# Another order for the opening of attention and for the casts of its keys

## The chip, the cores and the metric

The kernel runs on 1 core of one Trainium2 chip. The metric is the time of one execution in microseconds (us).

## What is computed

A block of three parts on x (4 batches, 128 tokens, width 512): cross attention over a context of 2048 tokens with 16 heads of 32, a gated scan, and a mixture of experts. The change is in the first part:

```python
q = x.reshape(B, T, H, d) * scale          # x is layer-normed; B 4, T 128, H 16, d 32
k = cond_k.reshape(B, S, H, d) * scale     # S 2048; keys and values are the same context
v = cond_v.reshape(B, S, H, d)
scores = jnp.einsum('bthd,bshd->bhts', q, k)
w = jax.nn.softmax(scores.astype(jnp.float32), axis=-1).astype(scores.dtype)
out = jnp.einsum('bhts,bshd->bthd', w, v).reshape(B, T, W)
return out @ w_proj.T + b_proj
```

## The kernel before

Attention works on 16 groups, one for each batch and block of four heads. A group's keys (1 MB, float32, `kt`, two buffers) are split into two float16 parts: ACT casts the high part (`kh`, two halves of two heads, `split_keys` at L433), and POOL subtracts it from the keys for the low part (`kl`, four heads, one instruction each, L608). DMAs from one place of SBUF to another then stack them for the matmuls, rows high, low, high, 32 rows each, in one of three stacks (`stacks[j % 3]`): six copies of 128 KB for each half `h` of the 2048 keys, so twelve for a group. The third stack lies in `wst[:, 1]`, where expert weights go later.

For each group PE then makes 16 matmuls of unscaled scores (`max_scores`, L1013) whose maxima DVE takes (L720; L772 for group 0); DVE makes the shift out of them; PE transposes queries with the shift in them (`shifted`, L1027), ACT copies them (`take_shifted`, L455); PE makes the scores in eight steps (`scores`, L1035), ACT the exponents (`exponent`, L470, four buffers), POOL sums each pair of key tiles (`pair_sum`, L632), and PE adds up values (`values`, L1049) and denominators from the pair sums (`denominators`, L1064).

Every engine has its own order, written out by hand, and waits on semaphores. All of them go in groups i of four quarters p of two steps each. In quarter p of group i PE makes maxima of group i+1 (in the last quarter of group i+2), scores of steps 2p+2 and 2p+3, which reach into the next group in the last quarter, then denominators of the two steps before the current ones, and values of steps 2p and 2p+1. `shifted(i+1)` stands on PE before the last quarter. ACT makes the exponents of PE's scores, in quarter 1 `take_queries(i+2)`, in quarter 2 `take_shifted(i+1)`, in quarter 3 `queries_high(i+3)`. ACT's casts of group i+3 stand in quarters 0 and 1 (in group 0: those of group 2 there, those of group 3 in quarters 2 and 3), and POOL's subtracts after pair sums 3 and 5 (in group 0: 5 and 7). For group 0 DVE makes the low parts of three heads, and for group 2 too, in the middle of its maxima (`low_parts`, L754).

Exponent n waits for `values(n-4)` and pair sum n-4, pair sum n for `denominators(n-4)`, scores n for exponent n-2. A cast of group j waits for its keys and for the copies of stack j-2; the high copies of a half wait for both casts, and from group 3 on for the scores that read the stack before; the low copies wait for POOL's last subtract of the group.

SP issues all these DMAs in one order. In the opening it issues first tokens, first keys, the identity, two rows of ones for the stacks, and the other tokens once the first keys are there; then the copies of stack 0, of which ACT issues the four high ones of half 1; then second keys, values of group 0, and so on.

Of the kernel before, what the change touches and what calls it, by code (L numbers as in the profile page):

```python
# [82 lines left out]
def build_program(nc, t, out):  # L83
# [240 lines left out]
    def stack_rows(eng, j, h, src, rows):  # L324
        for row in rows:
            for q in (2 * h, 2 * h + 1):
                eng.dma_start(stacks[j % 3][row:row + HD, :, q * S // 4:(q + 1) * S // 4],
                              src[q * HD:(q + 1) * HD, j % 2, :, :]).then_inc(k_rep[j % 3][h], 16)

    @blk.sync  # L330
    def _(sp):
        def load_k(j):
            if j >= 2:
                sp.wait_ge(split_lo, j - 1)
                sp.wait_ge(lo_dve, 2 * min(j // 2, 2))
            sp.dma_start(kt[:, j % 2, :, :], t["keysT"][j]).then_inc(kt_in[j % 2], 16)
# [6 lines left out]
        def copies(j, h, src, rows):  # L343
            stack_rows(sp, j, h, src, rows)

        def stack(j, h):
            sp.wait_ge(split_hi, 2 * j + 2)
            if j >= 3:
                sp.wait_ge(st_done, HS * (j - 3) + HS // 2 * (h + 1))
            copies(j, h, kh, (0, 2 * HD))  # L350
            sp.wait_ge(split_lo, j + 1)
            if j == 2:
                sp.wait_ge(lo_dve, 4)
            copies(j, h, kl, (HD,))
# [3 lines left out]
        sp.dma_start(idh[:, :], t["idh"]).then_inc(id_in, 16)  # L358
        sp.dma_start(kstk[KS:KM, :, :, :], t["ones"]).then_inc(ones_in, 16)
        sp.dma_start(stacks[2][KS:KM, :, :], t["ones"][:, 0, :, :]).then_inc(ones_in, 16)  # L360
        sp.wait_ge(kt_in[0], 16)
        sp.dma_start(x[:, 1:B, :], t["x"][:, 1:B, :]).then_inc(x_in, 16)
        sp.wait_ge(split_hi, 2)
        copies(0, 0, kh, (0, 2 * HD))
        sp.wait_ge(lo_dve, 2)
        sp.wait_ge(split_lo, 1)
        copies(0, 0, kl, (HD,))
        copies(0, 1, kl, (HD,))
        load_k(1)
        load_v(0)  # L370
        stack(1, 0)
        load_k(2)
        stack(1, 1)
        load_k(3)
        load_v(1)
        stack(2, 0)
        stack(2, 1)
        for i in range(G):
            if i + 4 < G:
                load_k(i + 4)  # L380
            if 0 < i < G - 1:
                load_v(i + 1)
            if i + 3 < G:
                stack(i + 3, 0)
                stack(i + 3, 1)
            if i == G - 3:
                for dst, name in CONSTS:
                    sp.dma_start(dst, t[name]).then_inc(consts, 16)
            if i == G - 2:
                for m in range(3):  # L390
                    sp.dma_start(wst[:, 0, m, :, :], t["ffw"][0, m]).then_inc(w_in[0][m], 16)
# [40 lines left out]
    def _(act):  # L432
# [51 lines left out]
        act.wait_ge(split_hi, 2)  # L484
        stack_rows(act, 0, 1, kh, (0, 2 * HD))
        queries_high(0)
        queries_high(1)
        take_queries(0)
# [3 lines left out]
        for h in range(2):  # L492
            split_keys(1, h)
# [4 lines left out]
        for i in range(G):  # L498
            for p in range(HS // 2):
                for n in scores_in(i, p):  # L500
                    exponent(n)
                if p == 1 and i + 2 < G:
                    take_queries(i + 2)
                if i == 0 and p < 2:
                    split_keys(2, p)
                if p in ((2, 3) if i == 0 else (0, 1)) and i + 3 < G:
                    split_keys(i + 3, p % 2)
                if p == 2 and i + 1 < G:
                    take_shifted(i + 1)
                if p == 3 and i + 3 < G:  # L510
                    queries_high(i + 3)
# [95 lines left out]
    def _(pool):  # L607
        def split_keys(j, a):  # L608
            if a % 2 == 0 or j in (0, 2):
                pool.wait_ge(split_hi, 2 * j + a // 2 + 1)  # L610
            low = pool.tensor_tensor(kl[:, j % 2, a, :], kt[:, j % 2, a, :], kh[:, j % 2, a, :], ALU.subtract)  # L611
            if a == HG - 1:
                low.then_inc(split_lo, 1)
# [11 lines left out]
        split_keys(0, HG - 1)  # L625
        queries_low(0)
        queries_low(1)
        for a in range(HG):
            split_keys(1, a)
# [15 lines left out]
        for i in range(G):  # L645
            for hs in range(HS):
                pair_sum(HS * i + hs)
                if i == 0 and hs == 4:
                    split_keys(2, HG - 1)
                if hs in ((5, 7) if i == 0 else (3, 5)) and i + 3 < G:  # L650
                    for a in ((0, 1) if hs == (5 if i == 0 else 3) else (2, 3)):
                        split_keys(i + 3, a)
                if hs == HS - 1 and i + 3 < G:
                    queries_low(i + 3)
# [49 lines left out]
    def _(dve):  # L704
# [49 lines left out]
        def low_parts(j, h):  # L754
            dve.wait_ge(split_hi, 2 * j + h + 1)
            heads = (slice(0, 2), slice(2, 3))[h]
            dve.tensor_tensor(kl[:, j % 2, heads, :], kt[:, j % 2, heads, :], kh[:, j % 2, heads, :], ALU.subtract)\
                .then_inc(lo_dve, 1)

        low_parts(0, 0)  # L760
        low_parts(0, 1)
# [23 lines left out]
        for i in range(G):  # L785
            if i == G - 1:
                scale_win()
            for p in range(HS // 2):
# [9 lines left out]
                if p in (1, 2) and i == 0:  # L798
                    low_parts(2, p - 1)
# [566 lines left out]
```

## Time and profile before

| | us |
|---|---|
| median of 3 runs | 535.68 |
| lowest and highest | 532.35, 535.93 |
| the profiled execution | 537.27 |
| its span in the profile | 535.5 |

| engine | busy us | share of the span |
|---|---|---|
| PE (matmuls) | 468.8 | 88% |
| DVE | 401.7 | 75% |
| ACT | 329.7 | 62% |
| POOL | 290.4 | 54% |

Attention ends at about 290 us, so POOL's busy time lies nearly all in the first 55% of the span. The profiled execution took 1.8 us more than the span, which begins with the first instruction and ends with the last.

### The profile page before, as it was taken

Reading aid. Unit: us, or ns where it says so; the run is one execution under the profiler, and the core shown is the slowest. Engines: PE = TensorE matmul, PEld = TensorE weight load, DVE = VectorE, ACT = ScalarE, POOL = GpSimd, SP = SyncE. Lnnn points to the kernel's source line nnn. Section 1 sums busy time; section 2 is a strip of 40 time slices with the busy share of each in tenths; the row PEclk is TensorE's granted clock in tenths of the full one; section 3 lists DMA queues with packets and bytes.
Section 4 is the critical chain, followed back from the end, with each engine's and each line's share of the span. In section 5 each row is a group of like instructions: output and inputs, shape, how many; then the busy total and the mean of one; then the engine's idle time right before and its main releaser. Section 6 shows DMA issues by size and latency. Waiting matters only on the chain.

```text
span 535.5 us, 15785 instructions
## 1 busy us (share of the span) xinstructions
PE 468.8 (88%) x6731; PEld 329.2 (61%) x6731; DVE 401.7 (75%) x598; ACT 329.7 (62%) x362; POOL 290.4 (54%) x274
## 2 busy tenths in 40 slices
PE   0468887999999999999989955999999999999994
PEld 0126555676666766667666532844878788787642
DVE  3467665787877788787771799698599999999426
ACT  3327465776767777776654373456579888788320
POOL 2045698899999999999769430482001101010042
PEclk9999898999999999999999996999999999999998
DMA  7986799878888987987992731076999999997125
GB/s 201 239 194 202 194 257 273 241 206 223 248 255 251 265 255 188 256 223 183 359 375 97 295 97 61 1 253 232 416 355 412 416 420 416 417 417 319 40 85 171
DMA packets 48253, 133.97 MB, mean 250 GB/s; under 512 B 6452, under 2 KB 31284, under 8 KB 37428
## 3 DMA queue, kind: packets, MB, share of 16 engines
q1 hardware_dynamic: 43928, 120.38, 69.3%
q0 software_dynamic: 3680, 12.06, 6.2%
q8 instruction: 53, 0.87, 0.7%
q10 hardware_dynamic: 576, 0.52, 0.5%
q14 instruction: 16, 0.13, 0.1%
HBM read 96.77 MB, written 11.01 MB: 201 GB/s over the span
## 4 chain that ended last, share of the span: by engine, by line
PE 45%; DVE 34%; DMA 8%; issue 8%; ACT 2%; POOL 2%; SPq 1%; DVEq 0%; ACTq 0%; POOLq 0%
DVE mx L720 11%; DVE ws L805 9%; PE bank L1059 8%; PE bank L1024 8%; PE bank L1068 6%; PE bank L1044 6%; DMA wst<-in_ffw 5%; PE bank L1186 2%; PE bank L1188 2%; DVE rden L737 2%; PE bank L1187 2%; DMA kstk<-kl 2%; DVE hf L946 1%; PE bank L1129 1%; DVE hl L951 1%
## 5 line engine op out<-in xcount | busy, mean ns | idle before, releaser
L720 DVE TENSOR_REDUCE mx<-bank 128x1 f32<-128x512 f32 x240 | 152.7, 686 | 60.2 <-PE bank L1024 60.0
L475 ACT ACTIVATE pt<-bank 128x1024 f32<-128x1024 f32 x128 | 126.0, 1023 | 70.8 <-PE bank L1044 69.5
L636 POOL TENSOR_TENSOR ps<-pt 128x512 f32<-128x512 f32 x128 | 159.8, 1275 | 14.8 <-PE bank L1068 9.2
L805 DVE SCALAR_TENSOR_TENSOR ws<-wst,ws 128x2048 f16<-128x2048 f32 x51 | 115.6, 2286 | 2.6 <-ACT ws L523 2.4
L523 ACT ACTIVATE ws<-wst 128x2048 f16<-128x2048 f32 x48 | 90.5, 1904 | 5.9 <-DMA wst<-in_ffw 5.7
L611 POOL TENSOR_TENSOR kl<-kt,kh 128x512 f16<-128x512 f32 x58 | 67.4, 1185 | 27.4 <-ACT kh L440 27.4
L1201 PE MATMUL bank<-xt,ws 128*128 128x128 f16 x480 | 81.2, 219 | 1.1 <-DVE hf L946 1.1
L1202 PE MATMUL bank<-xt,ws 128*128 128x128 f16 x480 | 81.2, 219 | 0.0
L1203 PE MATMUL bank<-xt,ws 128*128 128x128 f16 x480 | 81.2, 219 | 0.0
L1024 PE MATMUL bank<-kstk,q 96*128 96x512 f16 x176 | 66.6, 420 | 15.6 <-DMA kstk<-kl 7.5
L677 POOL DMA_DIRECT2D ys_rows<-xn x15 | 8.1, 543 | 121.7 <-ACT xn L592 121.7
L1059 PE MATMUL bank<-pt,v 128*32 128x128 f32 x2048 | 69.5, 277 | 2.9 <-issue 2.9
L1059 PEld LDWEIGHTS bank<-pt,v 128*32 128x32 f32 x2048 | 58.5, 112 | 3.7 <-issue 3.1
L1044 PEld LDWEIGHTS bank<-q,kstk 98*128 98x128 f16 x704 | 47.5, 101 | 15.9 <-issue 4.1
L1044 PE MATMUL bank<-q,kstk 98*128 98x128 f16 x704 | 55.7, 225 | 1.7 <-ACT pt L475 1.0
L1201 PEld LDWEIGHTS bank<-xt,ws 128*128 128x128 f16 x480 | 46.8, 98 | 2.0 <-DVE hf L946 2.0
L1203 PEld LDWEIGHTS bank<-xt,ws 128*128 128x128 f16 x480 | 46.9, 98 | 0.0
L1202 PEld LDWEIGHTS bank<-xt,ws 128*128 128x128 f16 x480 | 46.9, 98 | 0.0
L1068 PE MATMUL bank<-ps,ones 128*32 128x128 f32 x1024 | 41.8, 279 | 2.0 <-POOL ps L636 2.0
L440 ACT ACTIVATE kh<-kt 128x1024 f16<-128x1024 f32 x32 | 33.5, 1053 | 10.5 <-DMA kt<-in_keysT 10.5
L1024 PEld LDWEIGHTS bank<-kstk,q 96*128 96x128 f16 x176 | 15.3, 101 | 39.1 <-DVE mx L720 21.1
L1068 PEld LDWEIGHTS bank<-ps,ones 128*32 128x32 f32 x1024 | 24.1, 109 | 17.9 <-issue 12.2
(170 smaller groups left out, 719.0 us busy)
## 6 DMA issues: line engine op xcount, KB each, us to landing
wst<-in_ffw SPq DMA_DIRECT2D x51, 1024.0 KB, 11.0
kt<-in_keysT SPq DMA_DIRECT2D x16, 1024.0 KB, 6.3
v<-in_vals SPq DMA_DIRECT2D x16, 1024.0 KB, 9.7
kstk<-kh SPq DMA_DIRECT2D x84, 128.0 KB, 3.3
kstk<-kl SPq DMA_DIRECT2D x44, 128.0 KB, 2.8
wst<-kh SPq DMA_DIRECT2D x40, 128.0 KB, 2.8
xs_rows<-biases SPq DMA_DIRECT2D x15, 256.0 KB, 3.0
x_tok<-xs_rows POOLq DMA_DIRECT2D x15, 256.0 KB, 8.5
```

Source lines behind the costliest of these rows:

```text
L475: act.activation(pt[:, n % 4, :, :, :].rearrange("p j a t -> p (j a t)"), bank[:, 2 * (n % 2):2 * (n % 2) + 2, :].rearrange("p j n -> p (j ...
L523: act.activation(ws[:, home_of(q), 0, m, :, :].rearrange("p c n -> p (c n)"), wst[:, q % 2, m, :, :].rearrange("p c n -> p (c n)"), ACT.Co ...
L636: pool.tensor_tensor(ps2[:, n % 4, :, :], pt[:, n % 4, 0, :, :], pt[:, n % 4, 1, :, :], ALU.add)\
L720: dve.tensor_reduce(mx[:, a, q:q + 1], bank[:, 4 + k % 2, :], AX.X, ALU.max).then_inc(m_taken, 1)
L805: dve.scalar_tensor_tensor(ws[:, home_of(q), 1, m, :, :].rearrange("p c n -> p (c n)"), wst[:, q % 2, m, :, :].rearrange("p c n -> p (c n) ...
L1024: pe.matmul(bank[:, home, :], q1[:, j % 2, a, :], stacks[j % 3][0:KS, a, q * 512:(q + 1) * 512], start=True, stop=True).then_inc(m_ready, 1)
L1044: mm = pe.matmul(bank[:, 2 * (n % 2) + j, a * P:(a + 1) * P], stacks[i % 3][:, a, tile * P:(tile + 1) * P], q2[:, i % 2, a, :], start=True ...
L1059: mm = pe.matmul(bank[a * HD:(a + 1) * HD, 6 + i % 2, 0:P], v[:, i % 2, tile, a * HD:(a + 1) * HD], pt[:, n % 4, j, a, :], start=(tile == ...
L1068: mm = pe.matmul(bank[a * HD:(a + 1) * HD, 6 + i % 2, P:2 * P], ones[:, :], ps2[:, n % 4, a, :], start=False, stop=(hs == HS - 1), skip_gr ...
L1201: pe.matmul(o, ws[:, home, 0, m, c, part], xt[:, k % 2, c, :], start=(c == 0), stop=False)
L1202: pe.matmul(o, ws[:, home, 0, m, c, part], xt[:, k % 2, C + c, :], start=False, stop=False)
L1203: mm = pe.matmul(o, ws[:, home, 1, m, c, part], xt[:, k % 2, c, :], start=False, stop=(c == C - 1))
```

## The change

- SP: the other tokens and the second keys are issued right behind the first keys and the identity, with no wait. Then come the copies of stack 0, all twelve from SP, half 0 whole before half 1; then the rows of ones, the third keys, and the stacks, values and keys that follow. ACT issues no copies.
- Group 0's low parts: all four heads by DVE, two at a time. Group 1's and group 2's: all by POOL, before the first pair sum.
- ACT: the casts of group 1 come before `take_queries(0)`, those of group 2 before `take_shifted(0)`. In the groups, the casts of group i+3 come in quarter 2, behind `take_shifted(i+1)`, and in quarter 3, behind the exponents, in group 0 as in all.
- POOL: the subtracts of group i+3 come after pair sums 5 and 7.
- SP in the groups: values of group i+2 between the two halves of stack i+3, instead of values of group i+1 ahead of them. The constants go out three at a time in groups 4 to 7, and the first expert's weights in groups 8 to 10, instead of in groups 13 and 14.

```diff
@@ -321,18 +321,13 @@
     blk = block.__enter__()
 
 
-    def stack_rows(eng, j, h, src, rows):
-        for row in rows:
-            for q in (2 * h, 2 * h + 1):
-                eng.dma_start(stacks[j % 3][row:row + HD, :, q * S // 4:(q + 1) * S // 4],
-                              src[q * HD:(q + 1) * HD, j % 2, :, :]).then_inc(k_rep[j % 3][h], 16)
-
     @blk.sync
     def _(sp):
         def load_k(j):
             if j >= 2:
-                sp.wait_ge(split_lo, j - 1)
-                sp.wait_ge(lo_dve, 2 * min(j // 2, 2))
+                sp.wait_ge(split_lo, j - 2)
+            if j == 2:
+                sp.wait_ge(lo_dve, 2)
             sp.dma_start(kt[:, j % 2, :, :], t["keysT"][j]).then_inc(kt_in[j % 2], 16)
 
         def load_v(j):
@@ -341,54 +336,52 @@
             sp.dma_start(v[:, j % 2, :, :], t["vals"][j]).then_inc(v_in[j % 2], 16)
 
         def copies(j, h, src, rows):
-            stack_rows(sp, j, h, src, rows)
+            for row in rows:
+                for q in (2 * h, 2 * h + 1):
+                    sp.dma_start(stacks[j % 3][row:row + HD, :, q * S // 4:(q + 1) * S // 4],
+                                 src[q * HD:(q + 1) * HD, j % 2, :, :]).then_inc(k_rep[j % 3][h], 16)
 
         def stack(j, h):
             sp.wait_ge(split_hi, 2 * j + 2)
             if j >= 3:
                 sp.wait_ge(st_done, HS * (j - 3) + HS // 2 * (h + 1))
             copies(j, h, kh, (0, 2 * HD))
-            sp.wait_ge(split_lo, j + 1)
-            if j == 2:
-                sp.wait_ge(lo_dve, 4)
+            if j == 0:
+                sp.wait_ge(lo_dve, 2)
+            else:
+                sp.wait_ge(split_lo, j)
             copies(j, h, kl, (HD,))
 
         sp.dma_start(x[:, 0, :], t["x"][:, 0, :]).then_inc(x0_in, 16)
         load_k(0)
         sp.dma_start(idh[:, :], t["idh"]).then_inc(id_in, 16)
+        sp.dma_start(x[:, 1:B, :], t["x"][:, 1:B, :]).then_inc(x_in, 16)
+        load_k(1)
+        stack(0, 0)
+        stack(0, 1)
         sp.dma_start(kstk[KS:KM, :, :, :], t["ones"]).then_inc(ones_in, 16)
         sp.dma_start(stacks[2][KS:KM, :, :], t["ones"][:, 0, :, :]).then_inc(ones_in, 16)
-        sp.wait_ge(kt_in[0], 16)
-        sp.dma_start(x[:, 1:B, :], t["x"][:, 1:B, :]).then_inc(x_in, 16)
-        sp.wait_ge(split_hi, 2)
-        copies(0, 0, kh, (0, 2 * HD))
-        sp.wait_ge(lo_dve, 2)
-        sp.wait_ge(split_lo, 1)
-        copies(0, 0, kl, (HD,))
-        copies(0, 1, kl, (HD,))
-        load_k(1)
+        load_k(2)
+        stack(1, 0)
         load_v(0)
-        stack(1, 0)
-        load_k(2)
         stack(1, 1)
         load_k(3)
+        stack(2, 0)
         load_v(1)
-        stack(2, 0)
         stack(2, 1)
         for i in range(G):
             if i + 4 < G:
                 load_k(i + 4)
-            if 0 < i < G - 1:
-                load_v(i + 1)
             if i + 3 < G:
                 stack(i + 3, 0)
+            if i + 2 < G:
+                load_v(i + 2)
+            if i + 3 < G:
                 stack(i + 3, 1)
-            if i == G - 3:
-                for dst, name in CONSTS:
-                    sp.dma_start(dst, t[name]).then_inc(consts, 16)
-            if i == G - 2:
-                for m in range(3):
-                    sp.dma_start(wst[:, 0, m, :, :], t["ffw"][0, m]).then_inc(w_in[0][m], 16)
+            for dst, name in CONSTS[3 * i - 12:3 * i - 9] if 4 <= i < 8 else []:
+                sp.dma_start(dst, t[name]).then_inc(consts, 16)
+            if 8 <= i < 11:
+                sp.dma_start(wst[:, 0, i - 8, :, :], t["ffw"][0, i - 8]).then_inc(w_in[0][i - 8], 16)
         sp.wait_ge(st_done, HS * (G - 1))
         for m in range(3):
             sp.dma_start(wst[:, 1, m, :, :], t["ffw"][2, m]).then_inc(w_in[1][m], 16)
@@ -481,16 +474,16 @@
         for h in range(2):
             split_keys(0, h)
         root(ln1_var, 1, 0, 1)
-        act.wait_ge(split_hi, 2)
-        stack_rows(act, 0, 1, kh, (0, 2 * HD))
         queries_high(0)
         queries_high(1)
+        for h in range(2):
+            split_keys(1, h)
         take_queries(0)
         take_queries(1)
         root(ln1_var, B, 1, B)
         act.activation(r1[:, 1, 0:2], eps[:, :], ACT.Exp)
         for h in range(2):
-            split_keys(1, h)
+            split_keys(2, h)
         take_shifted(0)
         exponent(0)
         exponent(1)
@@ -501,12 +494,10 @@
                     exponent(n)
                 if p == 1 and i + 2 < G:
                     take_queries(i + 2)
-                if i == 0 and p < 2:
-                    split_keys(2, p)
-                if p in ((2, 3) if i == 0 else (0, 1)) and i + 3 < G:
-                    split_keys(i + 3, p % 2)
                 if p == 2 and i + 1 < G:
                     take_shifted(i + 1)
+                if p >= 2 and i + 3 < G:
+                    split_keys(i + 3, p - 2)
                 if p == 3 and i + 3 < G:
                     queries_high(i + 3)
 
@@ -606,7 +597,7 @@
     @blk.gpsimd
     def _(pool):
         def split_keys(j, a):
-            if a % 2 == 0 or j in (0, 2):
+            if a % 2 == 0:
                 pool.wait_ge(split_hi, 2 * j + a // 2 + 1)
             low = pool.tensor_tensor(kl[:, j % 2, a, :], kt[:, j % 2, a, :], kh[:, j % 2, a, :], ALU.subtract)
             if a == HG - 1:
@@ -622,11 +613,11 @@
             pool.wait_ge(xs_hi, j + 1)
             pool.tensor_tensor(z[:, :, 2 * HD:KS], q, z[:, :, 0:HD], ALU.subtract).then_inc(xs_lo, 1)
 
-        split_keys(0, HG - 1)
         queries_low(0)
         queries_low(1)
-        for a in range(HG):
-            split_keys(1, a)
+        for j in range(1, 3):
+            for a in range(HG):
+                split_keys(j, a)
         queries_low(2)
 
         def pair_sum(n):
@@ -645,10 +636,8 @@
         for i in range(G):
             for hs in range(HS):
                 pair_sum(HS * i + hs)
-                if i == 0 and hs == 4:
-                    split_keys(2, HG - 1)
-                if hs in ((5, 7) if i == 0 else (3, 5)) and i + 3 < G:
-                    for a in ((0, 1) if hs == (5 if i == 0 else 3) else (2, 3)):
+                if hs in (5, 7) and i + 3 < G:
+                    for a in range(hs - 5, hs - 3):
                         split_keys(i + 3, a)
                 if hs == HS - 1 and i + 3 < G:
                     queries_low(i + 3)
@@ -751,14 +740,11 @@
 
         dve.wait_ge(x0_in, 16)
         first_norm(0, 1)
-        def low_parts(j, h):
-            dve.wait_ge(split_hi, 2 * j + h + 1)
-            heads = (slice(0, 2), slice(2, 3))[h]
-            dve.tensor_tensor(kl[:, j % 2, heads, :], kt[:, j % 2, heads, :], kh[:, j % 2, heads, :], ALU.subtract)\
+        for h in range(2):
+            heads = slice(2 * h, 2 * h + 2)
+            dve.wait_ge(split_hi, h + 1)
+            dve.tensor_tensor(kl[:, 0, heads, :], kt[:, 0, heads, :], kh[:, 0, heads, :], ALU.subtract)\
                 .then_inc(lo_dve, 1)
-
-        low_parts(0, 0)
-        low_parts(0, 1)
         dve.wait_ge(roots, 1)
         link(dve.reciprocal(lnv[:, 2, 0:1], lnv[:, 0, 0:1]))
         first_normed(0)
@@ -795,8 +781,6 @@
                     first_normed(i // C + 1)
                 if p == 2 and i + 1 < G:
                     shift(i + 1)
-                if p in (1, 2) and i == 0:
-                    low_parts(2, p - 1)
         invert(G - 1)
         divide(G - 1)
```

## Rows read from the trace of the kernel before

**Rows 1.** Chain of waits: start us, us, what (`values(8i+2)` of groups 1, 4, 5, 13)
```profile
68.20 0.87 PE bank L1059 x32
...
120.02 0.87 PE bank L1059 x32
...
135.22 0.87 PE bank L1059 x32
...
256.75 0.87 PE bank L1059 x32
```

**Rows 2.** Windows: stretch, length, busy us (count) of PE PEld DVE ACT POOL, PEclk, DMA
```profile
131.00:146.19 15.19, 14.53 (x292) 10.45 (x284) 12.53 (x24) 11.14 (x14) 14.90 (x14) 1.00 0.84 241
```

**Rows 3.** Timeline, one steady group: start us, us, engine, line, operation
```profile
129.81 4.96 POOL L636 TENSOR_TENSOR ps<-pt 128x512 f32<-128x512 f32 x4
...
130.87 1.06 PE L1059 MATMUL bank<-pt,v 128*32 128x128 f32 x32
...
134.57 0.65 PE L1068 MATMUL bank<-ps,ones 128*32 128x128 f32 x16
134.73 2.46 POOL L611 TENSOR_TENSOR kl<-kt,kh 128x512 f16<-128x512 f32 x2
...
135.03 1.06 PE L1059 MATMUL bank<-pt,v 128*32 128x128 f32 x32
...
139.62 2.27 POOL L611 TENSOR_TENSOR kl<-kt,kh 128x512 f16<-128x512 f32 x2
...
139.88 0.60 ACT L459 ACTIVATE q<-bank 98x512 f16<-98x512 f16 x1 [0.78 <-PE bank L1031]
...
141.86 2.49 POOL L636 TENSOR_TENSOR ps<-pt 128x512 f32<-128x512 f32 x2
...
142.31 1.94 ACT L475 ACTIVATE pt<-bank 128x1024 f32<-128x1024 f32 x2 [1.84 <-PE bank L1044]
...
144.63 0.42 POOL L623 TENSOR_TENSOR xs<-xn,xs 128x128 f16<-128x128 f32 x1 [0.29 <-ACT xs L467]
```

**Rows 4.** Timeline of the opening
```profile
7.31 2.00 ACT L440 ACTIVATE kh<-kt 128x1024 f16<-128x1024 f32 x2 [5.06 <-DMA kt<-in_keysT]
...
12.58 2.54 SPq L327 DMA_DIRECT2D kstk<-kl  x4
...
15.16 0.61 SPq L336 DMA_DIRECT2D kt<-in_keysT  x1
...
21.76 7.96 PE L1024 MATMUL bank<-kstk,q 96*128 96x512 f16 x16 [7.53 <-DMA kstk<-kl]
...
25.18 2.00 ACT L440 ACTIVATE kh<-kt 128x1024 f16<-128x1024 f32 x2 [5.42 <-DMA kt<-in_keysT]
...
26.32 4.49 POOL L611 TENSOR_TENSOR kl<-kt,kh 128x512 f16<-128x512 f32 x4 [12.91 <-ACT kh L440]
...
34.13 1.12 PE L1044 MATMUL bank<-q,kstk 98*128 98x128 f16 x9 [0.78 <-ACT q L459]
```

**Rows 5.** Timeline of the fill: DVE, then PE
```profile
47.14 2.18 DVE L757 TENSOR_TENSOR kl<-kt,kh 128x1024 f16<-128x1024 f32 x1
...
49.98 0.39 PE L1024 MATMUL bank<-kstk,q 96*128 96x512 f16 x1 [1.11 <-DVE mx L720]
...
52.20 0.42 PE L1031 MATMUL bank<-idh,xs 128*98 128x128 f16 x4
55.66 0.59 PE L1024 MATMUL bank<-wst,q 96*128 96x512 f16 x2 [3.04 <-issue]
...
83.77 1.73 PE L1059 MATMUL bank<-pt,v 128*32 128x128 f32 x32 [2.85 <-issue]
```

**Rows 6.** Tile `v`, 0 to 100 us: issue to landing
```profile
DMA to landing us min/median/max: 9.7/11.9/12.9
```

**Rows 7.** Windows of the opening: columns as in rows 2, the last GB/s
```profile
4.00:6.00 2.00, 0.00 (x0) 0.00 (x0) 0.88 (x2) 0.00 (x0) 0.00 (x0) 1.00 1.00 413
...
16.00:18.00 2.00, 0.00 (x0) 0.00 (x0) 1.81 (x6) 0.05 (x1) 0.00 (x0) 1.00 1.15 211
```

## The prediction

> **What bounds the kernel now.** I read the chain of waits first, then the timeline of one steady group, then the opening and the fill. From about 100 us to 267 us the chain repeats the same lines each group. The 32 value matmuls of one place, `values(8i+2)`, start at 120.02 us for group 4 and at 256.75 us for group 13: (256.75 - 120.02) / 9 = 15.19 us per group [rows 1]. For group 1 the same place is at 68.20 us, so the twelve groups from 1 to 13 took 188.55 us where 12 x 15.19 = 182.3 would do. Thus 6.3 us of fill losses lie in groups 1 and 2. In a steady group PE is busy 14.53 us and POOL 14.90 us of 15.19 [rows 2]: two engines nearly full, and whatever makes one wait for the other lengthens the group. In the timeline of such a group [rows 3] POOL does four pair sums (129.81 to 134.73), two subtracts, two sums, two subtracts, two sums, and `queries_low`. Its casts on ACT came long before, so POOL hardly waits. The opening is another matter: PE starts its first maxima at 21.76 us, 7.53 us after its last work, released by the landing of the first stack's low rows [rows 4]. In the fill PE stands idle 3.04 us at 55.66 (the third stack's copies are late) and 2.85 us at 83.77 (values of group 2 loaded late) [rows 5].
>
> **The loop that the change closes (the steady groups).** This is the dear part. After the change ACT casts the first half of group i+3 behind `exponent(8i+6)`, `exponent(8i+7)` and `take_shifted(i+1)`; before, these casts stood in quarters 0 and 1. POOL's first two subtracts stand behind pair sum 5 and wait for that cast, and behind them are queued sums 6 and 7, two more subtracts, `queries_low` and the next group's sums. PE's denominators of the next group wait for these sums, and on PE the shifted transposes of the next group stand behind those denominators. So it comes back to the cast. I add up this loop from the rows of one steady group [rows 3]:
> - from the start of `values(8i+2)` at 135.03 to the start of `take_shifted` at 139.88: 4.85 us, PE busy throughout with matmuls that the change leaves as they are;
> - `take_shifted` 0.50 (it is listed at 0.60, and successive ACT starts overlap it a little), the cast 1.00 (two of them took 2.00 [rows 4]), the signal to POOL 0.07;
> - two subtracts 2.24 (start 139.62 to start 141.86), sums 6 and 7 2.49, two subtracts 2.24, `queries_low` 0.40, two sums of the next group 2.48 (half of 4.96);
> - the signal to PE 0.06, and the second half of the denominators 0.23 (half of 135.03 - 134.57; the first half is already done while the second sum runs), then `values` of the next group.
>
> The sum is 16.56 us; I take 16.6 against 15.19. The lower end is 16.3, if overlaps of starts save a little more. The upper end is 17.4: subtracts at 2.46 each pair as in the row at 134.73, both denominators behind the sum (0.46), ACT's pieces at full length. I stay near the low end because most rows of the loop are start-to-start distances already. With 16.6 the loop costs 12 x 1.41 = 16.9 us over groups 1 to 13 against a steady 15.19. The other users of the late pieces have room: the second cast (quarter 3) follows exponents that end at 144.25, so it is done at 145.3, before POOL asks at 146.2; `queries_low` ends at 148.8, and between the transposes that wait for it and the denominators, which wait until 151.4 anyway, PE has only three maxima and one set of scores, so a short delay there is covered.
>
> **SP's queue in the loop.** `load_v(i+2)` now stands behind the low copies of stack i+3, which wait for POOL's last subtract. On the scale of rows 3 that is 148.4 + 1.25 for two copies (half of 2.54 [rows 4]), so issue at 149.7. Its user, the first values of group i+2, comes at 130.9 + 2 x 16.6 = 164.1. A values load took 9.7 to 12.9 us to land [rows 6], so it lands by 162.6 at the latest: 1.5 us to spare, cost nil; if it took 15 us, each group would pay half of the excess, for two groups pass in between. `load_k(i+4)` has over a group of room. The constants (three a group in groups 4 to 7) and the first expert weights (groups 8 to 10) move out of a stretch where nobody waits for them into one where the queue has room: nothing either way.
>
> **The opening.** Removed: the wait of the other tokens and second keys for the first keys, ACT's four copies, DVE's share of group 2's subtracts. Added: group 2's casts and all four of its subtracts on POOL ahead of group 0, one longer subtract on DVE (two heads instead of one), whose end I leave where it is, since POOL no longer works beside it. Replayed:
> - First keys land and are cast 7.31 to 9.31 as now [rows 4]. Behind them in the queue are 0.77 MB of tokens and 1 MB of second keys. The queue moved 413 GB/s at 4 to 6 us [rows 7], which puts the second keys' end near 11.7 us and, with landing time, 12.5 to 14.
> - SP alone issues six copies of half 0 from 9.35, 0.63 us each (2.54 for four [rows 4]), so until 13.2. They stand behind the second keys, drain at about the 211 GB/s of 16 to 18 us [rows 7], 0.79 MB in 3.7 us from 11.7, and land by 16 to 17. Now twelve copies, tokens and all must land for the first maximum.
> - On ACT the second casts come ahead of `take_queries(0)`: cast at 13.5 to 15.5, queries at 16.0. Cost nil, covered by the copies; if the second keys came 1 us later it would show fully.
> - PE starts at 16.5 instead of 21.76: 5.2 us gained (bounds 3.5 and 6). Half 1 is issued by 17.0 and landed by 19.7, PE wants it 4.7 us after its start, 21.2.
> - Third keys are issued at 17.6 behind the rows of ones, and land at about 24 to 26 (the second keys took 10 us from 15.16 to the cast at 25.18 [rows 4]; fewer bytes are ahead of them now). Their casts take 2 us and stand ahead of `take_shifted(0)` on ACT, which is wanted some 0.7 us before `scores(0)`, at 28.2: covered, by as little as 0.2 us at worst. POOL's eight subtracts (4.49 for four [rows 4]) end near 30.5, before the first two exponents, for which POOL's next work waits.
>
> So `scores(0)`, now at 34.13 [rows 4], comes at 28.9.
>
> **Group 0.** DVE's subtract of 2.18 us at 47.14 goes; PE was idle 1.11 us for the maximum behind it at 49.98 [rows 5], so about 1.0 comes back. `shifted(1)`, now at 52.20 [rows 5], would be at 52.20 - 5.2 - 1.0 = 46.0. Here the new loop takes over: `take_shifted` from 46.5, cast end 48.0, subtracts 50.4, sums 52.8, subtracts 55.1, `queries_low` 55.5, two sums 58.0, denominators 58.25. The stall of 3.04 us on the third stack goes, since its subtracts end at 30.5 already; what is late instead is POOL. `values(8+2)` starts at 58.3; now it is at 68.0 on the same scale (the chain's 68.20 less the 0.19 by which the chain's 135.22 is behind the timeline's 135.03). That is 9.7 us gained by group 1. Values of group 2 are issued at about 56.5 and land by 69.4; PE wants them near 70.7, so the stall at 83.77 goes too.
>
> **The sum.** 58.3 + 12 x 16.6 = 257.5 us for group 13, against 256.75 - 0.19 = 256.56: +0.9 us. Behind that point the last three groups have no casts and the rest is untouched. The profiled execution lasted 537.27 us (span 535.5), 1.6 above the median 535.68 of the three runs; added to the median, the forecast is 536.6 us: two large effects, 16 us gained in opening and fill and 17 us lost in the loop, that nearly cancel.
>
> **The Trainium skill on one point.** The row of 4 to 6 us shows 413 GB/s with only first keys in the queue [rows 7], and no row shows two large loads of one queue started together. The Trainium skill ("DMA: Bandwidth & Descriptors", Queues, rings and completion order) says that on each DMA engine the descriptors of a ring are consumed in ring order. By that rule the first keys land as now; without it, see the third rival.
>
> **Rivals.**
> - The loop at its long end, slower. Where POOL's subtracts meet DVE work, and both denominators follow the sum, a group takes 17.1 to 17.4 us. From 17.0 on the change is over 1% slower (12 x 0.4 + 0.9 = 5.7). Price at 17.2: +8.1, so 543.8 us. For it: the subtract pair at 134.73 took 2.46 [rows 3]; against it: the later one took 2.24.
> - The loop does not bind, faster. If POOL's lag were absorbed and groups stayed at 15.19, group 13 would come at 58.3 + 182.3 = 240.6, so -16, 520 us. For it: four buffers of exponents lie between ACT and POOL; against it: every link above is an order in one engine or a wait.
> - The queue is shared, not in order. First keys, tokens and second keys end together: 2.8 MB at 413 GB/s is 6.8 us instead of 2.5, first cast 4.2 us later. Most of the opening's gain is gone, +4 or so: 540.7 us, still within 1%.
> - The second keys are later than I think and the gain of the opening halves: +2.5, 539.1 us.
>
> **Chances.** My forecast 0.40, the long loop 0.32, no loop 0.15, shared queue 0.07, late second keys 0.06. One per cent, about what a measurement of this kernel tells from no change, is 5.4 us. Faster by more: 0.15; within: 0.40 + 0.07 + 0.06 = 0.53; slower: 0.32. The range goes from 530 (a larger gain in the fill) to 546, and leaves out the case without the loop and the last of the long one.
>
> **What would show it.** The first maxima on PE near 16.5 us; no wait of 3 us at the third stack; POOL idle about 2 us before its first subtract of each group, put down to ACT's cast; that place in the chain 16.6 us apart, with `kl`, `ps` and `kh` on the chain where now maxima are. I am wrong if groups stay at 15.2, if values loads hold PE at a group's start, or if the first cast starts after 9 us.

## The result

The changed kernel takes 547.67 us (median of 6 runs) against 535.8 us: 1.022 times as long, 95% interval 1.0177 to 1.0262. The forecast was 536.6 us with a range to 546.0, so the change is slower by far more than the forecast's 0.9 us. One execution of each kernel took far longer than its others (696.35 us before, 1175.14 us changed), and the ratio is of the fast ones alone. The profiled execution of the changed kernel took 546.27 us, with a span of 544.5 against 535.5.

The chain of waits of the changed kernel, at the place that [rows 1] follow (`values(8i+2)`, now L1043; start us, us, what), in groups 1, 5, 6 and 13:

```profile
62.27 0.87 PE bank L1043 x32
...
128.43 0.87 PE bank L1043 x32
...
144.98 0.87 PE bank L1043 x32
...
266.62 0.87 PE bank L1043 x32
```

Group 1 reaches it at 62.27 us instead of 68.20 [rows 1]: the opening and the fill did gain, 5.9 us. A profile is one execution, though: in the profiles of two experiments whose opening is that of the kernel before, PE's first maxima start at 19.56 and 22.32 us instead of 21.76, so such a gain is known only to some 3 us. Then an undisturbed group takes 144.98 - 128.43 = 16.55 us instead of 15.19, and the twelve groups take 204.35 us instead of 188.55. At group 13 the changed kernel is 9.9 us behind; after that it wins 0.9 back.

The timeline of one such group shows where the time stands, to be laid beside [rows 3]:

```profile
125.48 7.59 POOL L627 TENSOR_TENSOR ps<-pt 128x512 f32<-128x512 f32 x6
...
134.71 2.27 POOL L602 TENSOR_TENSOR kl<-kt,kh 128x512 f16<-128x512 f32 x2 [1.64 <-ACT kh L433]
136.94 2.50 POOL L627 TENSOR_TENSOR ps<-pt 128x512 f32<-128x512 f32 x2
139.39 2.28 POOL L602 TENSOR_TENSOR kl<-kt,kh 128x512 f16<-128x512 f32 x2
...
133.09 0.60 ACT L452 ACTIVATE q<-bank 98x512 f16<-98x512 f16 x1 [0.78 <-PE bank L1015]
133.59 1.05 ACT L433 ACTIVATE kh<-kt 128x1024 f16<-128x1024 f32 x1
...
128.01 0.43 PE L1052 MATMUL bank<-ps,ones 128*32 128x128 f32 x8 [0.27 <-POOL ps L627]
128.25 1.06 PE L1043 MATMUL bank<-pt,v 128*32 128x128 f32 x32
```

POOL's first subtract stands idle 1.64 us for ACT's cast, which comes right behind `take_shifted`; and PE's second denominators wait for POOL's sum. Most links of the loop are in these rows: 128.25 to 133.09 is 4.84 us (4.85 in the working), the cast ends at 134.64, and 134.71 + 2.23 + 2.45 + 2.24 leads to `queries_low`. The rest of the ring is the same work as at 125.48 to 128.25, one group on.

The opening, to be laid beside [rows 4]:

```profile
7.33 2.00 ACT L433 ACTIVATE kh<-kt 128x1024 f16<-128x1024 f32 x2 [5.09 <-DMA kt<-in_keysT]
...
15.64 7.96 PE L1008 MATMUL bank<-kstk,q 96*128 96x512 f16 x16 [2.05 <-DMA kstk<-kl]
...
18.25 0.36 SPq L331 DMA_DIRECT2D kt<-in_keysT  x1
...
29.39 2.00 ACT L433 ACTIVATE kh<-kt 128x1024 f16<-128x1024 f32 x2 [12.64 <-DMA kt<-in_keysT]
...
32.02 1.87 PE L1028 MATMUL bank<-q,kstk 98*128 98x128 f16 x16 [4.79 <-ACT q L452]
```

The first cast starts at 7.33 us, as before, with 1.8 MB more in the queue behind the first keys: the queue isn't shared out. PE starts its maxima at 15.64 instead of 21.76. But the third keys, issued at 18.25, reach ACT only at 29.39, their casts hold up `take_shifted(0)`, and PE waits 4.79 us: of 6.1 us gained, 2.1 remain at `scores(0)`.

Last, four waits of PE that the engines' names don't explain (timeline of PE, "issue"; at the second one the 32 value matmuls are cut in two), and one group's window:

```profile
154.78 0.60 PE L1008 MATMUL bank<-wst,q 96*128 96x512 f16 x2 [1.84 <-issue]
...
168.57 0.83 PE L1043 MATMUL bank<-pt,v 128*32 128x128 f32 x23
170.56 0.49 PE L1043 MATMUL bank<-pt,v 128*32 128x128 f32 x9 [1.16 <-issue]
...
235.50 0.59 PE L1008 MATMUL bank<-kstk,q 96*128 96x512 f16 x2 [1.05 <-issue]
...
253.87 0.59 PE L1008 MATMUL bank<-wst,q 96*128 96x512 f16 x2 [2.53 <-issue]
```

```profile
242.13:262.11 19.98, 16.35 (x292) 11.86 (x284) 11.89 (x24) 11.11 (x15) 14.80 (x14) 0.91 0.81 204
```

Three of them stand before the first maxima on a new half stack, whose copies are late; the one at 170.56 is none of these, and the last section comes back to it. They lie in or right behind the groups in which SP issues constants (from 132 us on) or expert weights (at 217 and 233 us). The window, group 12 from one reciprocal (`invert`) to the next, is 19.98 us long, with a granted clock of 0.91: behind the wait of 2.53 us PE ran at 1.2 GHz for a while, here from 256 to 258 us, the column before the last two being the granted clock:

```profile
256.00:258.00 2.00, 2.00 (x29) 1.59 (x22) 0.00 (x0) 0.00 (x0) 1.72 (x2) 0.50 0.68 148
```

How late the queue was is told by the times from issue to landing, the last number of each line: first from 106.9 to 123.4 us, before any constant was issued, then from 208.3 to 242 us, among the weights:

```profile
kt<-in_keysT SPq DMA_DIRECT2D x1, 1024.0 KB, 8.4
kstk<-kl SPq DMA_DIRECT2D x4, 128.0 KB, 4.6
...
kt<-in_keysT SPq DMA_DIRECT2D x2, 1024.0 KB, 15.3
kstk<-kl SPq DMA_DIRECT2D x8, 128.0 KB, 7.5
```

### The profile page after: what moved, and what is told of

Same layout as the page of the kernel before. It is cut to its first block, busy times and chain, and to the rows that moved or that the text cites. A ratio compares the mean times of both kernels' runs of the same rounds, so it can differ in the third digit from the quotient of the medians.

```text
span 544.5 us, 15769 instructions
## 1 busy us (share of the span) xinstructions
PE 474.3 (87%) x6731; PEld 328.7 (60%) x6731; DVE 402.3 (74%) x596; ACT 329.4 (60%) x362; POOL 290.9 (53%) x276
## 4 chain that ended last, share of the span: by engine, by line
PE 40%; DVE 25%; POOL 11%; DMA 10%; issue 9%; SPq 3%; ACT 3%; DVEq 0%; POOLq 0%; ACTq 0%
DVE ws L789 9%; PE bank L1043 7%; DVE mx L709 6%; PE bank L1008 6%; POOL ps L627 6%; PE bank L1028 6%; PE bank L1052 5%; DMA wst<-in_ffw 5%; DMA kt<-in_keysT 3%; POOL kl L602 3%; SPq L341 2%; PE bank L1170 2%; PE bank L1171 2%; PE bank L1172 2%; DMA kstk<-kl 2%
## 5 line engine op out<-in xcount | busy, mean ns | idle before, releaser
L709 DVE TENSOR_REDUCE mx<-bank 128x1 f32<-128x512 f32 x240 | 153.9, 686 | 72.2 <-PE bank L1008 71.8
L1043 PE MATMUL bank<-pt,v 128*32 128x128 f32 x2048 | 70.2, 278 | 1.3 <-issue 1.2
L1043 PEld LDWEIGHTS bank<-pt,v 128*32 128x32 f32 x2048 | 58.9, 112 | 2.5 <-issue 1.8
L1052 PE MATMUL bank<-ps,ones 128*32 128x128 f32 x1024 | 46.1, 284 | 5.5 <-POOL ps L627 5.5
L433 ACT ACTIVATE kh<-kt 128x1024 f16<-128x1024 f32 x32 | 33.4, 1052 | 17.7 <-DMA kt<-in_keysT 17.7
L1052 PEld LDWEIGHTS bank<-ps,ones 128*32 128x32 f32 x1024 | 23.3, 110 | 26.2 <-POOL ps L627 12.3
```

Of the source, the lines that this page charges most:

```text
L709: dve.tensor_reduce(mx[:, a, q:q + 1], bank[:, 4 + k % 2, :], AX.X, ALU.max).then_inc(m_taken, 1)
L1043: mm = pe.matmul(bank[a * HD:(a + 1) * HD, 6 + i % 2, 0:P], v[:, i % 2, tile, a * HD:(a + 1) * HD], pt[:, n % 4, j, a, :], start=(tile == ...
L1052: mm = pe.matmul(bank[a * HD:(a + 1) * HD, 6 + i % 2, P:2 * P], ones[:, :], ps2[:, n % 4, a, :], start=False, stop=(hs == HS - 1), skip_gr ...
```

## The experiments

The length of group i is told by the distance of its reciprocals, `invert(i-1)` to `invert(i)`, which stand at its start and its end. In the kernel before they are 17.1 and 19.7 us for the first two and 15.19 after; in the changed one 16.5 to 16.6 up to group 12, but 18.9, 16.7, 16.1, 17.3 and 20.0 in groups 6, 7, 8, 11 and 12. The kernel before was timed again beside each set of experiments, and each ratio is to that, with medians of 536.05, 536.31, 535.93 and 536.85 us.

**Third keys ahead of the ones.** The changed kernel, with

```diff
-        ones rows (two loads)
         load_k(2)
+        ones rows (two loads)
```

> The changed kernel with the third keys issued ahead of the two rows-of-ones loads instead of behind them. Theory of the ones: their few long descriptors hold two of the DMA engines from 19.5 to some 24 us, and the third keys, which need all engines, land late (29.37 us) only for that. Then the keys land at 25 to 26 us, the first scores start at 28.7 instead of 32.02 us, and the whole is 2 to 3.5 us faster. Rival, plain backlog of stack copies in the queue: the keys move by the 1 us that they are issued earlier, and the whole by less than 1 us.

541.61 us, ratio to before 1.0065 (1.0021 to 1.0109): 6 us off the changed kernel. The keys landed after 6.1 us instead of 11.1:

```profile
23.64 2.00 ACT L433 ACTIVATE kh<-kt 128x1024 f16<-128x1024 f32 x2 [6.74 <-DMA kt<-in_keysT]
27.36 0.60 ACT L452 ACTIVATE q<-bank 98x512 f16<-98x512 f16 x1 [1.72 <-PE bank L1015]
28.11 1.87 PE L1028 MATMUL bank<-q,kstk 98*128 98x128 f16 x16 [0.78 <-ACT q L452]
```

`scores(0)` came at 28.11 us instead of 32.02. The ones are 96 KB only, but in rows of 32 and 16 KB on two partitions. The theory of the ones stands and the plain backlog falls. That the gain exceeds the 3.9 us of the opening isn't explained by it: the long groups came out shorter too in this run (17.7, 17.9 at most), though the constants were still among them: groups 1 to 12 took 200.7 us where the changed kernel's took 204.8. Why is open; the nine executions of this run are spread from 536.9 to 548.7 us.

**Constants late.** The changed kernel, with

```diff
-            for dst, name in CONSTS[3 * i - 12:3 * i - 9] if 4 <= i < 8 else []:
...
-            if 8 <= i < 11:
...
+            if i == G - 3:
+                for dst, name in CONSTS:
...
+            if i == G - 2:
+                for m in range(3):
...
```

> The changed kernel with the constants and the first expert's weights issued where they were before the change (groups 13 and 14). Theory: in the groups they push stack copies and loads back in a DMA queue that is nearly full, and cost the 5.8 us by which groups 1 to 13 exceed 12 x 16.55 us. Then every group from 1 to 13 takes 16.55 us and the whole is 5 to 6 us faster. Rival: the waits of 1 to 2.5 us in groups 6, 8, 11 and 12 come from stack copies that the loop itself makes late; then they stay and the time changes by under 1 us.

543.75 us, ratio 1.016 (1.0111 to 1.0209), 4 us faster than the changed kernel. Groups 1 to 12 took 199.4 us instead of 204.8 between the first reciprocal and the thirteenth: 5.4 us, as expected of the groups; the whole gained less than the expected 5 to 6. Single groups of 17.0 and 17.4 us stayed, against the expectation, and each holds a stop of PE inside a run of matmuls, 0.65 and 1.09 us, of which more in the last section. The profiled run began 1 us later and lost the rest behind attention.

**Casts early.** The changed kernel, with ACT's casts of groups 1 to 12 in quarters 0 and 1 and POOL's subtracts after pair sums 3 and 5 again.

```diff
+                if p in ((2, 3) if i == 0 else (0, 1)) and i + 3 < G:
+                    split_keys(i + 3, p % 2)
                 if p == 2 and i + 1 < G:
                     take_shifted(i + 1)
-                if p >= 2 and i + 3 < G:
-                    split_keys(i + 3, p - 2)
...
-                if hs in (5, 7) and i + 3 < G:
+                if hs in ((5, 7) if i == 0 else (3, 5)) and i + 3 < G:
```

> The changed kernel with the casts and subtracts of groups 1 to 12 where they were before the change (ACT quarters 0 and 1, POOL after pair sums 3 and 5); group 0 and all else as changed. Theory of the loop (cast behind take_shifted, sums behind the subtracts): groups fall from 16.55 to 15.2 us, 12 x 1.36 = 16 us faster, less up to 4 us that the constants cost more in shorter groups: 531 to 535 us. Rival, the longer groups come from the DMA queue (loads and copies late): groups stay near 16.5 us and the gain is under 3 us.

545.85 us, ratio 1.0191 (1.0116 to 1.0266): only 1.8 us gained. The rival has the number, under 3 us, but neither theory had the groups right. Groups of 15.18 and 15.19 us did appear, so the loop is gone; but beside them stood groups of 20.7, 18.7 and 20.6 us. The chain of waits names one cause in group 10:

```profile
197.31 19.22 DMA kt<-in_keysT
```

The keys of a later group took 19.22 us behind twelve copies, values and a weight, and ACT, which now casts in quarter 0, stood before them with all exponents behind it. In group 4, before any constant is issued, the cause is another:

```profile
115.92 1.05 PE L1043 MATMUL bank<-pt,v 128*32 128x128 f32 x31
119.35 0.37 PE L1043 MATMUL bank<-pt,v 128*32 128x128 f32 x1 [2.38 <-issue]
```

PE stops between the 31st and the 32nd of 32 matmuls that no wait divides. Nine such stops add up to 9.3 us in this run; I come back to them below.

**Casts late in the kernel before.** The opposite edit: the kernel before, with this part of the change alone: the diff above, its signs turned round.

> The kernel before with one part of the change alone: casts of groups 1 to 12 in ACT quarters 2 and 3 and subtracts after pair sums 5 and 7. Theory of the loop: from group 3 on each group takes 16.55 instead of 15.19 us, ten groups of 1.36 us, 13 to 15 us slower, near 549.5 us. Rival, the DMA queue: loads and constants stand as before, so the time stays near 536 us.

552.04 us, ratio 1.0238 (1.0155 to 1.0321), 16 us slower, a little more than expected. The chain repeats every 16.55 us here too:

```profile
121.19 0.87 PE bank L1059 x32
...
137.74 0.87 PE bank L1059 x32
...
154.30 0.87 PE bank L1059 x32
```

So the loop alone, with loads and constants in their old places, makes the group 1.36 us longer, 13.6 us over ten groups. Most of the rest of the 16 us lies in group 7, which took 19.6: PE waits there 2.49 us for values.

**Subtracts after sum 7.** The changed kernel, with all four subtracts of a group behind `pair_sum(8i+7)`: it shortens the loop by sums 6 and 7 without moving a cast.

```diff
-                if hs in (5, 7) and i + 3 < G:
-                    for a in range(hs - 5, hs - 3):
+                if hs == 7 and i + 3 < G:
+                    for a in range(HG):
                         split_keys(i + 3, a)
```

> The changed kernel with all four subtracts of a group after pair sum 7, so that sums 6 and 7 no longer stand behind the first cast; the casts stay late. Theory of the loop, added up from its links: take_shifted ends 6.35 us after the values of quarter 1, POOL subtracts from the first cast's end, waits for the second cast until some 10.2 us after that mark, then two subtracts, queries_low, two sums and the denominators: 15.8 to 16.0 us a group instead of 16.55, so 6 to 8 us faster than the changed kernel unless the DMA queue gives some of it back. Rival, the cast alone sets the length: 16.55 stays.

541.85 us, ratio 1.0046 (0.9996 to 1.0097). Undisturbed groups took 15.65 us, 0.15 less than the low end I had added up and 0.9 less than with the loop of the change. POOL waits for each half's cast, as the sum had it:

```profile
99.30 2.27 POOL L602 TENSOR_TENSOR kl<-kt,kh 128x512 f16<-128x512 f32 x2
102.48 2.28 POOL L602 TENSOR_TENSOR kl<-kt,kh 128x512 f16<-128x512 f32 x2 [0.91 <-ACT kh L433]
104.72 0.42 POOL L614 TENSOR_TENSOR xs<-xn,xs 128x128 f16<-128x128 f32 x1
```

The loop's length follows its links; one group of 22.2 us among the constants remained.

**Three parts undone.** The changed kernel with the diffs of three experiments together: third keys ahead, constants late, casts early.

> The changed kernel with three parts undone together: third keys ahead of the rows of ones, constants and first weights late, casts and subtracts of groups 1 to 12 early. What is left of the change is the opening, group 0, and the place of the values load between two stack halves. If the constants made the long groups (up to 20.7 us) of the early casts, groups take 15.2 to 15.5 us and the whole is 522 to 526 us. Rival, the place of the values load makes copies, keys and instruction fetches late in a group of 15.2 us: several groups stay at 17 us or more and the whole is 530 us or more.

533.14 us, ratio 0.9945 (0.9902 to 0.9988). The rival came true in the time, 530 us or more, and half way in the groups: they took 15.19 us, but also 16.4, 16.8, 17.6 and 18.5. Stops of PE inside runs of matmuls add up to 4.7 us here, a wait for copies makes 2.3.

**Constants in the groups of the kernel before.** The kernel before, with the diff of "constants late" turned round.

> The kernel before with the constants and first weights in groups 4 to 10, as in the change, and nothing else. Theory, a nearly full DMA queue: the groups of 15.19 us that get 1 MB or more in addition become longer, 3 to 8 us in all, 539 to 544 us. Rival, the queue has room (as the prediction had it): all groups stay at 15.19 and the time at 536 us.

543.43 us, ratio 1.0079 (1.0034 to 1.0125). Six groups kept 15.18 to 15.20 us; four among the loads took 19.2, 16.3, 16.8 and 16.5, and one ahead of them 16.6, with a stop of 0.96 us inside a run. The first group that took in constants, from 127.20 to 142.40 us, is among the six: 1.5 MB more went through at 307 GB/s with no loss. The loss came in the next:

```profile
144.59 1.77 PE L1057 MATMUL bank<-pt,v 128*32 128x128 f32 x32 [2.27 <-issue]
```

The values for this place were issued at 131.61, behind the constants and the keys, and took 12.9 us to land. So the queue can take 1 MB more into one group; what is issued behind it and waited for comes late.

**Only the opening.** As "three parts undone", and with the values load back ahead of both stack halves:

```diff
+            if 0 < i < G - 1:
+                load_v(i + 1)
             if i + 3 < G:
                 stack(i + 3, 0)
-            if i + 2 < G:
-                load_v(i + 2)
-            if i + 3 < G:
                 stack(i + 3, 1)
```

> As the run with three parts undone, with the values load of a group back in its old place ahead of both stack halves: SP's order in the groups is that of the kernel before, and only the opening and group 0 are changed. Theory, the place of the values load matters: groups of 15.19 us from group 1 or 2 on, the first reciprocal near 55 us instead of 63.9, two groups of fill at most 1 us too long, in all 519 to 523 us. Rival, groups become long for the shorter lead of the fill itself: then this run has long groups as well and stays above 526 us.

528.06 us, ratio 0.9833 (0.9769 to 0.9896): the fastest of all, 8 us faster than the kernel before and 20 faster than the changed one. All groups from 4 on took 15.19 us:

```profile
106.56 0.96 DVE rden L727
...
121.75 0.96 DVE rden L727
```

The steady groups are as the theory has them, but the time is on the rival's side, above 526 us. It is 5 us slower than I expected: the first reciprocal came at 57.85, not 55, and the first three groups took 3.1 us too long. It is a version that beats both kernels; it isn't the end of the road.

**Opening and loop.** The last kernel with the late casts put back.

> The run with only the opening changed (528.1 us), with the late casts and subtracts of groups 1 to 12 put back and nothing else. Theory: the loop costs 12 x 1.36 = 16.3 us by itself, whatever the queue does; every group takes 16.55 us and the time is 543 to 546 us. Rival, the loop's cost depends on loads and constants in the queue: with these in their old places the groups are shorter than 16.4 us.

544.43 us, ratio 1.0115 (1.004 to 1.019): 16.4 us more than with early casts by the medians, 14.4 without the longest of the four executions. The expected number is 16.3, but it isn't shown that the loop alone makes it. In the profiled execution, that longest one (555.4; the others took 540 to 546), most groups took 16.55 us and three took 20.6 to 22.1, which neither side had:

```profile
163.24 1.93 PE L1044 MATMUL bank<-pt,v 128*32 128x128 f32 x32 [2.22 <-issue]
```

The values for this place were issued at 153.9 and took 9.2 us: they landed at 163.1. The wait of 2.49 us in "casts late in the kernel before" is at the same place. With late casts a values load that is issued behind both halves of a stack, which is itself late, comes too late.

**Values first, in the changed kernel.** The diff of "only the opening" alone, on the changed kernel.

> The changed kernel with the values load put back in its old place, ahead of both stack halves, and nothing else. In groups of 16.55 us the queue has more room than in groups of 15.19, so if the constants alone make the long groups of the changed kernel (18.9, 20.0 us), they stay and the time moves by less than 2 us; if the place of the values load has its part in them, they shrink and 3 us or more come back.

561.24 us, ratio 1.0402 (1.0322 to 1.0483). 13.6 us slower than the changed kernel, which I had on neither side:

```profile
146.37 1.94 PE L1042 MATMUL bank<-pt,v 128*32 128x128 f32 x32 [6.72 <-issue]
```

Issued at 134.0 behind constants of 1.5 MB and keys of 1 MB, the values landed 12.3 us later, at 146.3. So the new place of the values load is what late casts need, and the old place is what early ones need; each part of the change reads differently beside the other.

**Keys first and constants late, loop kept.** The first two diffs together on the changed kernel.

> The changed kernel with third keys ahead of the rows of ones and constants late: the loop and the values load between the stack halves stay. Theory: with the values load in its new place no group waits for values (groups of 20.6 and 22.1 us in the run with late casts and values first came from that), so nearly all of groups 1 to 12 take 16.55 us, one or two up to 1 us more; the sum of both single edits, 547.7 - 6 - 4, gives 538 to 541 us. Rival, the values' place is no cure: groups of 20 us appear here too.

538.97 us, ratio 1.0043 (1.0009 to 1.0076). Nine of the first twelve groups took 16.54 to 16.56 us, the others 16.1, 17.3 and 17.4. Two of its reciprocals, in DVE's timeline:

```profile
171.22 0.96 DVE L728 RECIPROCAL rden<-bank 128x128 f32<-128x128 f32 x1 [0.35 <-PE bank L1054]
...
187.76 0.96 DVE L728 RECIPROCAL rden<-bank 128x128 f32<-128x128 f32 x1 [0.37 <-PE bank L1054]
```

With both moved loads back in better places, the change is 2 us slower than the kernel before beside it: near the +0.9 of the forecast. Two of the long groups, 17.4 and 17.3 us, hold stops of PE of 0.98 and 1.03 us inside a run.

## Why the prediction was wrong

- **The loop**: right, and to the hundredth. 16.56 us added up, 16.55 measured; 16.6 was taken. Single links are off by up to 0.05 and cancel, which is luck in the last digit. Its ends (to 17.4) were too wide: none of the dear ends applied. The rival "no loop" falls with the groups of 16.55 us, in the kernel before too once its casts are late.
- **The opening up to the maxima**: right in kind, PE at 15.64 against 16.5. Queue in order: right, 7.33 against 7.31 us before. The Trainium skill's rule ("DMA: Bandwidth & Descriptors", Queues, rings and completion order) holds here.
- **"Third keys ... land at about 24 to 26"**: this step failed. They reached ACT at 29.39. I counted bytes ahead of them, and missed that the rows of ones, now just ahead, lie on two partitions. It cost 3.1 us at `scores(0)` (32.02 against 28.9). Shown by the first experiment, which gives back 3.9 us there and, by the medians, 6 us of the whole.
- **Group 0**: `values(8+2)` came 3.8 us late. In the first experiment it comes at 59.82 us in the chain instead of 62.27, so about 2.5 of them are the keys'. The other 1.3 I can't place.
- **"The constants ... and the first expert weights move ... into one where the queue has room: nothing either way"**: this step failed. In the profiled execution the twelve groups from 1 to 13 took 204.35 us, 5.1 more than 12 x 16.6 and 5.8 more than 12 x 16.55, and the trace of "constants late" gives 5.4 back. In whole time, by the medians, the loads cost 3.9 us in the changed kernel, 2.6 beside early third keys (541.61 against 538.97) and 7.1 in the kernel before (by the ratios 3, 1 and 4). So that they cost something is shown from both sides; how much depends on what stands beside them. Nor are all 5.1 us theirs: the stop of 1.16 us in group 7 is of another kind, and with the third keys ahead the same groups took 200.7 us with the constants in them and 199.8 without.
- **How that step failed**: I looked for room in the queue and didn't ask what is waited for behind the loads. A sum of bytes wouldn't have helped. The row of windows says 0.84 of the DMA engines' time in a steady group, in its last but one column [rows 2]; 1 MB more is 2.5 us at 413 GB/s [rows 7], and 0.84 x 15.19 + 2.5 is 15.3 us, an estimate, which fits into a group of 16.55. And the groups that took a load in did fit: 16.54 us with a weight in it (from 208.29 us, 272 GB/s), 15.20 with 1.5 MB of constants in the kernel before. The loss came behind, where keys landed after 15.3 us instead of 8.4 and low copies after 7.5 instead of 4.6, and PE waited 1.84, 1.05 and 2.53 us for copies.
- **SP's queue, values load "cost nil"**: right for the change as it stands; the experiments show by how little.
- **The sum**: +0.9 us forecast at group 13, +9.9 measured; 3.8 and 5.1 make the difference. The chances put 0.47 on two rivals of the loop, which came out as added up, 0.13 on the queue in the opening, and none on the rows of ones or the constants. The rival of the long loop names a time nearer to the measured one, 543.8 us, but by groups of 17.2 us, and the undisturbed ones took 16.55: its nearness is luck.

## What to carry to other kernels

Where an engine is moved behind a wait, add up the ring of waits that it closes: that sum, from start-to-start distances in one steady group, gave the group's length here to 0.01 us. For the DMA queue such a sum of bytes isn't enough to call a load free: look at each DMA behind it that an engine waits for, how long it takes to land, and how long its user can wait. Keep small loads to few partitions behind, not ahead of, a load that is waited for. And where several parts move, test them in pairs. With third keys ahead and constants late, the four kernels took 528.06 us (casts and values load in the old places), 533.14 (values load moved), 544.43 (casts moved) and 538.97 (both moved): the new place of the values load costs 5 us beside early casts and gives 5 back beside late ones.

## What was unexpected

**Few partitions, long rows.** Two loads of 64 and 32 KB to two partitions made 1 MB behind them land in 11.1 us instead of 6.1. The trace of the changed kernel has them as two packets of 32 KB, which took 2.6 and 2.1 us, each followed with no gap by one of 16 KB, which took 1.8. I read that as two of the 16 DMA engines being held for about 4 us each, near the 5.0 us by which the keys were late.

**PE stops inside a run of matmuls.** Gaps of 0.2 to 2.4 us lie between matmuls with no wait between them, at 23 + 9 of 32 in the changed kernel and at the same place in four of the experiments. The profile's DMA queues list one of kind "instruction" with 53 packets. In "casts early", in the stretch from 107.3 to 128 us around the stop of 2.38 us, it moved three packets beside a full data queue:

```profile
q1 hardware_dynamic: 2218, 4.43, 97.1%
q8 instruction: 3, 0.05, 1.2%
```

One of the three went from 116.63 to 117.92 us, and PE, which had stopped at 116.97, went on at 119.35. It is so each time: from 40 to 300 us the traces hold 30 such stops of 0.2 us and more, in nine kernels, and in all 30 PE goes on 1.3 to 1.7 us after an instruction packet has ended. So I read these gaps as PE's program coming late through the same DMA engines. The timing speaks for it strongly, but no run takes the cause away. The timeline of the kernel before shows none in attention, and that of the one with only the opening changed a single one, of 0.85 us. In sum they are 1.2 us in the changed kernel, 2.5 in "constants late", 4.7 in "three parts undone" and 9.3 in "casts early". Why some kernels have many and others none stays open.
